# Position bias: for every second group of tiles the first layer is a sum of two small tables, made on GpSimd

## The chip, the cores and the metric

The kernel runs on one core of a Trainium2 chip. The metric is the device time of one execution in microseconds (us). The engines are called PE (TensorE), DVE (VectorE), ACT (ScalarE), POOL (GpSimd) and SP (SyncE, which issues most DMAs here).

## The reference, cut to what matters

Four network layers are computed one after the other. The change touches only the first, an attention with deformed sampling and a learned position bias. The bias of a query pixel (y, x) towards a key position j goes through a small network of three layers with 128 channels:

```python
pos = grid_q[:, :, None, :] - grid_kv[:, None, :, :]
bias = jnp.sign(pos) * jnp.log1p(jnp.abs(pos))
bias = jax.nn.relu(bias @ cpb_w1 + cpb_b1)      # 2 -> 128
bias = jax.nn.relu(bias @ cpb_w2 + cpb_b2)      # 128 -> 128
bias = (bias @ cpb_w3 + cpb_b3).reshape(b, GROUPS, H * W, Hd * Wd)
```

There are 2 x 8 groups with 64 keys each, so 1024 keys, and 32 x 32 query pixels: about a million positions. Since `pos` has one part that depends on x alone and one that depends on y alone, the first layer before its rectification is the sum of a function of x and a function of y, for each key and channel.

## The kernel before, in words

`layer0_sampling` computes the key positions. DVE builds the differences U (L333), ACT takes their absolute value, logarithm and sign (L234 to L237), and DVE multiplies (L337) and splits the result into three bf16 parts (L342 to L351), which are added up as rows of POS, with POSX for the x axis. At the same time POOL makes products for the sampling (L149).

`layer0_bias` is the stage of the change. A tile is 128 channels x 512 positions: one key and one half of the pixels. Four tiles are a quad (their four keys lie in the four row groups of 32 partitions), and eight quads (32 tiles, 16 keys) are an iteration; there are 64 iterations. In each quad:

- PE makes the first layer for four tiles with four products of 32 rows each, into the four banks of z1 (L479). They read EXP, which POOL fills with one addition for four quads, the "spread" (L430).
- ACT rectifies each z1 tile, rounded, into R1 (L547, `first_part`), and DVE makes the rest, the rectified z1 less R1, into R2 (L572, `second_part`). R1 and R2 are rings of eight tiles.
- PE makes the second layer of a tile with three products (L492, L493, L495) into one of three banks of z2. Before the first it waits until the tile three before it has left its bank.
- z2 is rectified into H2 by ACT (L553) for three tiles of a quad and by DVE (L598) for the third one (t % 4 == 2).
- PE makes the third layer of the quad before (L504, or L513 for the last quad of an iteration), with its results gathered in one bank, zo. Once an iteration DVE reads it out (L578), and SP stores it (L444).

The order of PE in a quad is written out by hand: second layer of the quad's four tiles, third layer of the quad before, then the first layer of the quad two further on, which waits until DVE has made the second parts of the next quad (r2_ready). ACT and DVE work one quad ahead with the first and second parts. On ACT a quad is: first parts of t+4 and t+5, hidden tile t, first parts of t+6 and t+7, hidden tiles t+1 and t+3. On DVE it is: second parts of t+4 to t+7, hidden tile t+2.

Ahead of the loop, POOL makes two spreads and clears W3W (L461) and H2 (L462); DVE then fills W3W's windows (L588); and PE starts the third layer's bank with products of zeros (L522). SP loads the weights of the second layer (L447) and then prefetches 9 MB for later stages.

## Time and profile before

| | us |
|---|---|
| median of 3 runs | 4471.59 |
| lowest and highest of them | 4470.86, 4475.02 |
| the profiled execution, its own time | 4470.45 |
| its span in the profile | 4468.6 |

The page gives the busy time of each engine and its costliest groups; a line number is a line of the kernel. A row of the timeline has the start and the duration in microseconds, the engine, the line, the operation, output<-inputs, the shapes and how many instructions are merged in it, with the idle time before it in brackets. A row of one line's instructions has its shortest, median and longest duration in nanoseconds. The position bias takes the span from about 175 to 2380 us, nearly half of it.

### The profile page before, as it was taken

The numbers are of one execution on the slowest core, as the hardware profiler recorded it, in microseconds if no ns is written. First come the engines' busy times: TensorE is split into PE (matmuls) and PEld (weight loads), VectorE is DVE, ScalarE is ACT, GpSimd is POOL, SyncE is SP. The second block draws the span as 40 slices with busy tenths as digits, with TensorE's granted clock in tenths as the row PEclk, the third lists the DMA queues.
The fourth block names the chain that finished last, engine by engine and source line by source line (L and its number), as shares of the span: only waits on it lengthen the run. The fifth ranks groups of instructions, "written<-read, shape, count | busy, mean of one in ns | idle before, by whom it ended". The sixth has DMA issues, their size and how long they took to land. (4 is left out here: it accounts for less than half of the span.)

```text
span 4468.6 us, 65255 instructions
## 1 busy us (share of the span) xinstructions
PE 3954.4 (88%) x19432; PEld 2398.8 (54%) x19432; DVE 2971.8 (67%) x4247; ACT 2532.4 (57%) x4506; POOL 1223.0 (27%) x848
## 2 busy tenths in 40 slices
PE   2599999999999999999998999669878356969999
PEld 1355555555555555555555777537666232435553
DVE  7777777777777777777776333366888944235552
ACT  3488888888888888888885333222211220113331
POOL 1411111111111111111111445405667610016663
PEclk7799999999999999999999999889889666989999
DMA  1200000000000000000002000118999821363311
GB/s 44 86 2 2 2 2 2 2 2 2 2 2 2 2 2 2 2 2 2 2 2 77 1 0 0 65 41 320 377 376 374 309 82 49 125 155 67 67 39 76
DMA packets 136115, 309.13 MB, mean 69 GB/s; under 512 B 43400, under 2 KB 44424, under 8 KB 135004
## 3 DMA queue, kind: packets, MB, share of 16 engines
q1 hardware_dynamic: 94556, 157.02, 11.3%
q0 software_dynamic: 41472, 151.01, 8.7%
q8 instruction: 47, 0.77, 0.1%
q14 instruction: 40, 0.33, 0.0%
HBM read 228.83 MB, written 78.91 MB: 69 GB/s over the span
## 5 line engine op out<-in xcount | busy, mean ns | idle before, releaser
L572 DVE SCALAR_TENSOR_TENSOR cpb_r<-cpb_z,cpb_r 128x512 fp32r<-128x512 f32 x2052 | 1321.8, 686 | 491.8 <-ACT cpb_r L547 486.0
L547 ACT ACTIVATE cpb_r<-cpb_z 128x512 fp32r<-128x512 f32 x2052 | 1121.1, 604 | 278.0 <-PE cpb_z L479 278.0
L553 ACT ACTIVATE cpb_h<-cpb_z,net_vec 128x512 f32<-128x512 f32 x1536 | 1020.5, 714 | 2.0 <-PE cpb_z L495 2.0
L492 PE MATMUL cpb_z<-cpb_r,cpb_w2a 128*128 128x512 f32 x2048 | 856.7, 418 | 3.0
L493 PE MATMUL cpb_z<-cpb_r,cpb_w2b 128*128 128x512 f32 x2048 | 803.6, 392 | 0.0
L495 PE MATMUL cpb_z<-cpb_r,cpb_w2a 128*128 128x512 f32 x2048 | 797.4, 389 | 0.0
L430 POOL TENSOR_TENSOR cpb_exp<-l0k_posx,l0k_pos 128x1024 bf16 (+1 forms) x130 | 247.6, 1905 | 1966.3 <-PE cpb_z L479 1947.0
L1365 DVE SCALAR_TENSOR_TENSOR dc_acc<-dc_g,dc_wt,dc_acc 128x512 f32<-128x512 f32 x560 | 459.2, 826 | 52.4 <-DMA dc_g<-conv_out,dc_idx 36.9
L492 PEld LDWEIGHTS cpb_z<-cpb_r,cpb_w2a 128*128 128x128 f32 x2048 | 384.1, 188 | 189.8 <-issue 123.3
L504 PE MATMUL cpb_zo<-cpb_h,cpb_w3w 128*32 128x512 f32 x3584 | 477.3, 605 | 0.0
L495 PEld LDWEIGHTS cpb_z<-cpb_r,cpb_w2a 128*128 128x128 f32 x2048 | 385.3, 188 | 85.3
L493 PEld LDWEIGHTS cpb_z<-cpb_r,cpb_w2b 128*128 128x128 f32 x2048 | 385.6, 188 | 61.1
L1099 POOL DMA_INDIRECT dc_g<-conv_out,dc_idx x288 | 326.4, 1133 | 203.1 <-DVE dc_acc L1365 121.0
L598 DVE TENSOR_SCALAR cpb_h<-cpb_z,net_vec 128x512 f32<-128x512 f32 x512 | 379.4, 741 | 0.1
L1245 ACT COPY dc_ys<-dc_py 128x512 f32<-128x512 f32 x144 | 84.6, 588 | 384.6 <-DMA conv_out<-dc_ys 228.0
L1155 PE MATMUL dc_py<-net_conv_w,dc_dh 128*128 128x512 f32 x576 | 234.8, 408 | 65.1 <-ACT dc_ys L1245 57.7
L2013 ACT ACTIVATE net_x<-sa_pb 128x512 f32<-128x512 f32 x256 | 139.2, 595 | 267.8 <-PE sa_pb L1939 267.8
L479 PEld LDWEIGHTS cpb_z<-cpb_exp,l0k_w1p 32*128 32x128 bf16 x2056 | 51.9, 91 | 435.9 <-DVE cpb_r L572 430.7
L1909 POOL TENSOR_TENSOR sa_acc<-sa_acc,net_x 128x512 f32<-128x512 f32 x192 | 240.9, 1278 | 70.9 <-ACT net_x L2013 70.1
L885 POOL TENSOR_TENSOR mlp_wb<-l_w,mlp_wa 128x512 fp32r<-128x512 f32 x128 | 194.4, 1539 | 181.8 <-ACT mlp_wa L844 181.8
L2028 DVE TENSOR_REDUCE sa_mxp<-sa_pa 128x1 f32<-128x512 f32 x224 | 144.3, 685 | 147.9 <-PE sa_pa L1923 147.9
L1156 PE MATMUL dc_py<-net_conv_w,dc_dh 128*128 128x512 f32 x576 | 232.8, 404 | 0.0
(320 smaller groups left out, 4884.8 us busy)
## 6 DMA issues: line engine op xcount, KB each, us to landing
conv_out<-dc_ys SPq DMA_DIRECT2D x576, 64.0 KB, 6.2
qk_parts<-gn_r SPq DMA_DIRECT2D x64, 256.0 KB, 2.0
dc_wr<-in_dc_wT SPq DMA_DIRECT2D x9, 1024.0 KB, 5.9
bias_dram<-cpb_bst SPq DMA_DIRECT2D x520, 8.0 KB
net_x<-in_x SPq DMA_DIRECT2D x8, 1024.0 KB, 8.7
sa_qa<-qk_parts SPq DMA_DIRECT2D x16, 512.0 KB
sa_ka<-qk_parts SPq DMA_DIRECT2D x16, 512.0 KB
dc_g<-conv_out,dc_idx POOLq DMA_INDIRECT x288, 7.9
```

Source lines behind the costliest of these rows:

```text
L430: eng.tensor_tensor(EXP[:, slot].rearrange("p (y x) -> p y x", x=W), POSX[:, group, :].broadcast_to([P, H, W]), POS[:, group, :].rearrange ...
L492: pe.matmul(z2[:, bank, :], W2A[:], R1[:, k, :], start=True, stop=False)
L493: pe.matmul(z2[:, bank, :], W2B[:], R1[:, k, :], start=False, stop=False)
L495: pe.matmul(z2[:, bank, :], W2A[:], R2[:, k, :], start=False, stop=True).then_inc(z2_ready, 1)
L504: mm = pe.matmul(zo[32 * r:32 * r + 32, :], W3W[:, half * 4 + c, :], H2[:, (quad * 4 + r) % 8, :], start=(quad == 0), stop=False)
L547: act.activation(R1[:, t % RING, :], z1[:, t % 4, :], ACT.Relu).then_inc(r1_ready, 1)
L553: act.activation(H2[:, t % 8, :], z2[:, t % 3, :], ACT.Relu, bias=V("cpb_b2")).then_inc(h2a, 1)
L572: v.scalar_tensor_tensor(R2[:, t % RING, :], z1[:, t % 4, :], 0.0, R1[:, t % RING, :].bitcast(F32), ALU.max, ALU.subtract).then_inc(r2_rea ...
L598: v.tensor_scalar(H2[:, (t + 2) % 8, :], z2[:, (t + 2) % 3, :], V("cpb_b2"), 0.0, ALU.add, ALU.max).then_inc(h2v, 1)
L1099: pool.indirect_dma_start(out=G[:, u % GR, y, :], out_offset=None, in_=table[tap % SLOTS][b], in_offset=bass.IndirectOffsetOnAxis(ap=IDX[: ...
L1365: v.scalar_tensor_tensor(o, G[:, u % GR, k // 2, (k % 2) * C:(k % 2 + 1) * C], WT[:, k, col:col + 1], DCB[:] if tap == 0 and k == 0 else o ...
L1909: pool.tensor_tensor(acc, ET[:, 0, u, :] if k == 1 else acc, ET[:, k, u, :], ALU.add).then_inc(added, 1)
```

## The change

Quads 0, 2, 4 and 6 of an iteration keep the product on PE. For quads 1, 3, 5 and 7 the tile before the rectification is made on POOL: `SUM[c, y, x] = TAB_x[c, x] + TAB_y[c, y]`, a 128x512 f32 addition with both operands broadcast. The steps:

- In the sampling stage the logarithms stay in U[0] (the split goes on in U[1]), and SP stores their y rows for all keys to DRAM (`log_dram`) with eight DMAs.
- For each iteration SP loads the 16 rows that it needs, broadcast over all 128 partitions, into LOG (256 KB). POOL makes tables from it, by two small operations for each half of an iteration (slot): times the weight of x plus the bias, and times the weight of y.
- Four sums for each odd quad follow on POOL. SUM has the same place in SBUF as R2: a sum's slot may be written once the second layer of the tile that used the slot is complete (z2_ready). Then ACT reads the sum, and DVE reads it and R1, and writes R2 over the sum.
- The order on POOL in an iteration is: sums of quad 3, spread of slot 0, sums of quad 5, table of slot 0, sums of quad 7, spread of slot 1, sums of the next iteration's quad 1, table of slot 1. Ahead of the loop there are two tables and the sums of quad 1, before the two clears.
- PE's first layer is made for even quads only, with no wait for r2_ready. The order of the quads in an iteration (half, slot, j) is changed, so that odd quads are those of the second key half j.

```diff
+            sp.wait_ge(pos_step, 6)
+            for r in range(4):
+                for a in range(2):
+                    row = 32 * r + 16 + 8 * a
+                    sp.dma_start(g["log_dram"].rearrange("n r a x -> r a n x")[r, a].unsqueeze(0), U[0][row:row + 1]
+                                 ).then_inc(log_out, 16)
...
-                    v.tensor_tensor(U[0], U[0], UB[:], ALU.subtract).then_inc(pos_step, 1)
+                    v.tensor_tensor(U[1], rest, UB[:], ALU.subtract).then_inc(pos_step, 1)
...
-        R1, R2 = s.sb("r1", [P, RING, NF], F32R), s.sb("r2", [P, RING, NF], F32R)
+        R1 = s.sb("r1", [P, RING, NF], F32R)
+        with ExitStack() as room:
+
+            SUM = Scope(nc, room, "cpb").sb("sum", [P, RING, NF])
+        R2 = s.sb("r2", [P, RING, NF], F32R)
+        LOG, TAB = s.sb("log", [P, 2, 4, 2, W]), s.sb("tab", [P, 2, 4, 2, W])
...
-            c, half = divmod(quad, 2)
-            return half, c // 2, c % 2, c
+            slot, rest = divmod(quad, 4)
+            half, j = divmod(rest, 2)
+            return half, slot, j, slot * 2 + j
+
+        def on_pe(t):
+
+            return t // 4 % 2 == 0
+
+        def first_layer(t):
+            return z1[:, t % 4, :] if on_pe(t) else SUM[:, t % RING, :]
...
+            def logs(i):
+
+                sp.dma_start(LOG[:], g["log_dram"][i].rearrange("(o s) r a x -> o (s r a x)", s=2).broadcast_to([P, 512])
+                             .rearrange("p (s r a x) -> p s r a x", s=2, r=4, a=2)).then_inc(log_in, 16)
+
             sp.dma_start(W2F[:], d["cpb_w2"]).then_inc(w_in, 16)
+            logs(slice(0, 2))
+            sp.wait_ge(tables, 2)
+            logs(slice(2, 4))
             g["prefetch"](sp)
             with sp.Fori(0, ITERS) as i:
                 sp.wait_ge(staged, i + 1)
                 store(bass.ds(i, 1))
+                sp.wait_ge(tables, i * 2 + 4)
+                logs(bass.ds((i + 2) % ITERS * 2, 2))
...
+            def table(slot):
+
+                pool.nop(nofuse=True)
+                pool.tensor_scalar(TAB[:, slot, :, 0, :], LOG[:, slot, :, 0, :], V("cpb_w1", 0), V("cpb_b1"),
+                                   ALU.mult, ALU.add).then_inc(table_step, 1)
+                pool.tensor_scalar(TAB[:, slot, :, 1, :], LOG[:, slot, :, 1, :], V("cpb_w1", 1), None, ALU.mult
+                                   ).then_inc(tables, 1)
+
+            def sums(i, quad, table_count, consumed):
+
+                half, slot, _, _ = quad_of(quad % QUADS)
+                pool.wait_ge(table_step, table_count)
+                pool.wait_ge(tables, table_count)
+                for r in range(4):
+                    if consumed is not None:
+                        pool.wait_ge(z2_ready, consumed + r)
+                    pool.tensor_tensor(SUM[:, 4 + r, :].rearrange("p (y x) -> p y x", x=W),
+                                       TAB[:, slot, r, 0, :].unsqueeze(1).broadcast_to([P, NF // W, W]),
+                                       TAB[:, slot, r, 1, half * 16:half * 16 + 16].unsqueeze(2).broadcast_to([P, NF // W, W]),
+                                       ALU.add).then_inc(sum_ready, 1)
+
             for slot in range(2):
                 spread(pool, slice(slot, slot + 1), slot)
+            pool.wait_ge(log_in, 16)
+            table(0)
+            table(1)
+            sums(0, 1, 1, None)
             pool.memset(W3W[:], 0.0).then_inc(win_zero, 1)
             pool.memset(H2[:, 4:8, :], 0.0).then_inc(win_zero, 1)
...
-                pool.wait_ge(z1_ready, i * QUADS + QUADS // 2)
+                sums(i, 3, i * 2 + 1, i * TPI + 5)
+                pool.wait_ge(z1_ready, i * 4 + 2)
                 spread(pool, bass.ds(nxt * 2, 1), 0)
-                pool.wait_ge(z1_ready, i * QUADS + QUADS)
+                sums(i, 5, i * 2 + 2, i * TPI + 13)
+                pool.wait_ge(log_in, i * 16 + 32)
+                pool.wait_ge(sum_ready, i * 16 + 8)
+                table(0)
+                sums(i, 7, i * 2 + 2, i * TPI + 21)
+                pool.wait_ge(z1_ready, i * 4 + 4)
                 spread(pool, bass.ds(nxt * 2 + 1, 1), 1)
+                sums(i, 9, i * 2 + 3, i * TPI + 29)
+                pool.wait_ge(sum_ready, i * 16 + 16)
+                table(1)
...
-            pe.wait_ge(r2_ready, 4)
-            layer1(1)
...
-                    if quad + 2 == QUADS // 2:
-                        pe.wait_ge(exp_ready, i * 2 + 2)
-                    if quad + 2 == QUADS:
-                        pe.wait_ge(exp_ready, i * 2 + 3)
-                    pe.wait_ge(r2_ready, i * TPI + quad * 4 + 8)
-                    layer1((quad + 2) % QUADS)
+                    if quad % 2 == 0:
+                        if quad + 2 == QUADS // 2:
+                            pe.wait_ge(exp_ready, i * 2 + 2)
+                        if quad + 2 == QUADS:
+                            pe.wait_ge(exp_ready, i * 2 + 3)
+                        layer1((quad + 2) % QUADS)
...
-                act.activation(R1[:, t % RING, :], z1[:, t % 4, :], ACT.Relu).then_inc(r1_ready, 1)
+                act.activation(R1[:, t % RING, :], first_layer(t), ACT.Relu).then_inc(r1_ready, 1)
...
-                v.scalar_tensor_tensor(R2[:, t % RING, :], z1[:, t % 4, :], 0.0, R1[:, t % RING, :].bitcast(F32),
+                v.scalar_tensor_tensor(R2[:, t % RING, :], first_layer(t), 0.0, R1[:, t % RING, :].bitcast(F32),
                                        ALU.max, ALU.subtract).then_inc(r2_ready, 1)
```

## Rows read from the trace of the kernel before

**Rows 1.** The page's first part: busy time, share of the span, instructions.
```profile
PE 3954.4 (88%) x19432; PEld 2398.8 (54%) x19432; DVE 2971.8 (67%) x4247; ACT 2532.4 (57%) x4506; POOL 1223.0 (27%) x848
```

**Rows 2.** Stretches: length, busy PE, PEld, DVE, ACT, POOL, PE clock, DMA share, GB/s.
```profile
1000.00:2000.00 1000.00, 998.60 (x5612) 569.17 (x5611) 775.71 (x1198) 890.41 (x1637) 112.35 (x59) 1.00 0.01 2
```

**Rows 3.** Timeline of PE in one quad and the start of the next.
```profile
999.98 0.50 PE L492 MATMUL cpb_z<-cpb_r,cpb_w2a 128*128 128x512 f32 x1
...
1000.56 0.39 PE L495 MATMUL cpb_z<-cpb_r,cpb_w2a 128*128 128x512 f32 x1
...
1002.93 1.07 PE L504 MATMUL cpb_zo<-cpb_h,cpb_w3w 128*32 128x512 f32 x8
...
1003.93 0.40 PE L479 MATMUL cpb_z<-cpb_exp,l0k_w1p 32*128 32x512 bf16 x4
...
1004.25 0.50 PE L492 MATMUL cpb_z<-cpb_r,cpb_w2a 128*128 128x512 f32 x1
...
1005.05 0.40 PE L492 MATMUL cpb_z<-cpb_r,cpb_w2a 128*128 128x512 f32 x1
```

**Rows 4.** ACT in the same quad, and the page's group of a copy from SBUF.
```profile
1000.11 1.09 ACT L547 ACTIVATE cpb_r<-cpb_z 128x512 fp32r<-128x512 f32 x2 [0.47 <-PE cpb_z L479]
...
1002.60 1.30 ACT L553 ACTIVATE cpb_h<-cpb_z,net_vec 128x512 f32<-128x512 f32 x2
...
L844 ACT CAST mlp_wa<-l_w 128x512 fp32r<-128x512 f32 x128 | 72.7, 615 | 0.0
```

**Rows 5.** DVE in the same quad, and the durations of all of L572.
```profile
1000.74 1.29 DVE L572 SCALAR_TENSOR_TENSOR cpb_r<-cpb_z,cpb_r 128x512 fp32r<-128x512 f32 x2 [0.76 <-ACT cpb_r L547]
...
1003.50 0.74 DVE L598 TENSOR_SCALAR cpb_h<-cpb_z,net_vec 128x512 f32<-128x512 f32 x1
...
L572 DVE SCALAR_TENSOR_TENSOR cpb_r<-cpb_z,cpb_r x2052: 678/683/692, 181.4 to 2376.5; 128x512 fp32r<-128x512 f32 x187
```

**Rows 6.** POOL's spreads: two on the timeline, and all of the line.
```profile
195.96 1.90 POOL L430 TENSOR_TENSOR cpb_exp<-l0k_posx,l0k_pos 128x1024 bf16 x1 [15.19 <-PE cpb_z L479]
...
1000.27 1.91 POOL L430 TENSOR_TENSOR cpb_exp<-l0k_posx,l0k_pos 128x1024 bf16 x1 [15.06 <-PE cpb_z L479]
...
L430 POOL TENSOR_TENSOR cpb_exp<-l0k_posx,l0k_pos x130: 1901/1904/1979, 174.9 to 2369.6; 128x1024 bf16 x128, 128x1024 bf16<-128x1024 bf16 x2
```

**Rows 7.** POOL's additions of 512 f32: one line's durations, two in a row.
```profile
L1909 POOL TENSOR_TENSOR sa_acc<-sa_acc,net_x x192: 1256/1278/1298, 4012.6 to 4401.6; 128x512 f32<-128x512 f32 x192
...
2454.91 2.52 POOL L885 TENSOR_TENSOR mlp_wb<-l_w,mlp_wa 128x512 fp32r<-128x512 f32 x2
```

**Rows 8.** Timeline of DVE and POOL where both read two SBUF inputs; L902's durations.
```profile
140.50 6.44 DVE L348 SCALAR_TENSOR_TENSOR l0k_pos<-smp_ub,net_vec,l0k_pos 128x4096 bf16<-128x4096 bf16 x1
142.62 6.56 POOL L149 TENSOR_TENSOR net_x<-smp_hx,smp_hya 128x1024 f32<-128x1024 f32 x1
...
157.85 4.49 DVE L348 SCALAR_TENSOR_TENSOR l0k_pos<-smp_ub,net_vec,l0k_pos 128x4096 bf16<-128x4096 bf16 x1
...
2449.85 1.73 POOL L885 TENSOR_TENSOR mlp_wb<-l_wo,mlp_wa 128x512 fp32r<-128x512 f32 x1
...
2450.36 1.77 DVE L902 TENSOR_TENSOR mlp_ab<-l_q,mlp_aa 128x512 fp32r<-128x512 f32 x1
2451.54 1.72 POOL L885 TENSOR_TENSOR mlp_wb<-l_wo,mlp_wa 128x512 fp32r<-128x512 f32 x1
...
L902 DVE TENSOR_TENSOR mlp_ab<-l_q,mlp_aa x16: 679/1546/1772, 2448.1 to 2771.4; 128x512 fp32r<-128x512 f32 x16
```

**Rows 9.** Timeline ahead of the loop: POOL, DVE and PE.
```profile
176.80 0.23 DVE L581 CAST cpb_w2a<-cpb_w2f 128x128 fp32r<-128x128 f32 x1 [2.16 <-DMA cpb_w2f<-in_cpb_w]
...
178.72 0.31 POOL L461 MEMSET cpb_w3w<- 128x256 f32 x1
...
178.97 1.80 POOL L462 MEMSET cpb_h<- 128x2048 f32 x1
...
184.50 0.80 PE L492 MATMUL cpb_z<-cpb_r,cpb_w2a 128*128 128x512 f32 x1
```

More of the change, by code:

```diff
@@ L113, in layer0_sampling @@
         W1B = s.sb("w1b", [P, 3, P], BF16)
+        log_out = s.sem("log_out")
         pos_step, pos_abs, pos_ln, pos_sgn, w1_step = (s.sem("pos_step"), s.sem("pos_abs"), s.sem("pos_ln"),
@@ L135, in _ @@
             sp.dma_start(W1F[:], d["w1rows"]).then_inc(w_in, 16)
+            sp.wait_ge(pos_step, 6)
[4 more added lines that the diff above has]
+                                 ).then_inc(log_out, 16)
+            sp.wait_ge(log_out, 16 * 8)
         @block.gpsimd
@@ L340, in _ @@
             for part in range(3):
+                rest = U[min(part, 1)]
                 v.wait_ge(pos_step, n)
-                v.tensor_copy(UB[:], U[0]).then_inc(pos_step, 1)
+                v.tensor_copy(UB[:], rest).then_inc(pos_step, 1)
                 n += 1
@@ L403, in layer0_bias @@
         h2_free = s.sem("h2_free")
+        log_in, table_step, tables, sum_ready = s.sem("log_in"), s.sem("table_step"), s.sem("tables"), s.sem("sum_ready")
         staged = s.sem("bias_staged")
@@ L454, in _ @@
             sp.wait_ge(stored, 16 + 128 * (ITERS + 1))
+            sp.wait_ge(log_in, 16 * (ITERS + 2))
             g["prefetch_done"](sp)
@@ L544, in first_part @@
             def first_part(i, t):
-                if t % 4 == 0:
-                    act.wait_ge(z1_ready, i * QUADS + t // 4 + 1)
-                act.activation(R1[:, t % RING, :], z1[:, t % 4, :], ACT.Relu).then_inc(r1_ready, 1)
+                if not on_pe(t):
+                    act.wait_ge(sum_ready, i * (TPI // 2) + t // 8 * 4 + t % 4 + 1)
+                elif t % 4 == 0:
+                    act.wait_ge(z1_ready, i * (QUADS // 2) + t // 8 + 1)
+                act.activation(R1[:, t % RING, :], first_layer(t), ACT.Relu).then_inc(r1_ready, 1)
             def hidden(i, t):
@@ L2143 @@
 WEIGHT_COLUMNS = [("bn1_g", 4), ("bn1_b", 4), ("bn2_g", 4), ("bn2_b", 4), ("out_b", 4), ("mlp_b1", 16), ("mlp_b2", 4),
-                  ("off_dw_b", 1), ("off_dw_w", 36), ("off_pw_w", 2), ("cpb_b2", 1), ("cpb_w3", 1), ("cpb_b3", 1),
+                  ("off_dw_b", 1), ("off_dw_w", 36), ("off_pw_w", 2), ("cpb_b2", 1), ("cpb_w3", 1), ("cpb_b3", 1), ("cpb_w1", 2), ("cpb_b1", 1),
                   ("pw_b", 4), ("off_b", 1), ("dw_w", 18), ("dw_b", 2), ("a_dw_w", 18), ("a_dw_b", 2), ("a_pw_b", 4),
@@ L2206, in lay_out @@
          "off_pw_w": both(i["L0_off_pw_w"].T), "cpb_b2": i["L0_cpb_b2"].reshape(P, 1), "cpb_w3": i["L0_cpb_w3"].reshape(P, 1),
-         "cpb_b3": every(i["L0_cpb_b3"]),
+         "cpb_b3": every(i["L0_cpb_b3"]), "cpb_w1": i["L0_cpb_w1"].T, "cpb_b1": i["L0_cpb_b1"].reshape(P, 1),
          "off_b": np.concatenate([np.pad(i["L1_off_b"], (0, 14)).reshape(32, 1)] * 4),
@@ L2254, in build @@
             g["W1P"] = k.sb("w1p", [P, 2, P], BF16, side="right")
+            g["log_dram"] = nc.dram_tensor("log_dram", (P, 4, 2, W), F32).ap()
             layer0_sampling(nc, d, g)
```

## The prediction

> **What bounds the kernel now.** I read the page's busy shares first, then the stretches of time, then the costliest groups of instructions, and last the timeline of two quads, engine by engine. PE is busy for 88% of the span [rows 1]. Inside the position bias it is busy for 998.60 of 1000 us, at the full clock (PEclk 1.00), while DVE has 776, ACT 890 and GpSimd (POOL) 112 [rows 2]. A busy PE need not be a late PE, so the timeline must confirm it. A quad (4 tiles) begins with the first second-layer product (L492) at 999.98 and the next at 1004.25, 4.27 us later; in it PE runs 12 second-layer products, then the third layer (L504) from 1002.93, then the first layer (L479) of a later quad from 1003.93 to 1004.25 [rows 3]. There is no hole between these. So here a microsecond taken off PE is a microsecond gained, as long as no other engine is late.
>
> How late may they be? ACT works through 4 rectifications (L547) and 3 hidden activations (L553), is done at 1003.90, and has waited 0.47 us for the first layer before it began [rows 4]. DVE makes 4 second parts (L572, about 0.60 us apart) and one hidden tile (L598), done at 1004.24 [rows 5]. That last one matters: z2 has 3 banks, so PE's second tile of the next quad (L492 at 1005.05 [rows 3]) waits for it. It comes 0.81 us ahead of its use. POOL only makes one spread in two quads of four (L430), 1.90 us each, and waits 15 us between them [rows 6].
>
> The spreads begin at 195.96 and 2369.6, with 127 distances of four quads between [rows 6]: 2173.6 / 127 = 17.115 us, or 34.23 us for an iteration of 8 quads; there are 64 iterations.
>
> **What PE loses.** In each of the 4 odd quads of an iteration the group L479 goes. From its start to the next L492 is 0.32 us (1003.93 to 1004.25 [rows 3]); I use 0.33 for the small changes at the edge of the loop. 4 x 0.33 = 1.32 us, so PE alone would take 32.91 us for an iteration. This is 64 x 1.32 = 84 us for the kernel. The first L492 behind the group lasts 0.50 where the next lasts 0.40 [rows 3]; whether this 0.10 stays I can't see. So the bounds for a group are 0.22 and 0.42 us: 56 and 108 us in all.
>
> The Trainium skill (TensorE: Matmul & The Clock Gate, Part 3, "Measured speedup vs the span model") gives four row tiles one product's duration plus 4 ns a tile; with the 216 ns that the page gives for the gap of 512 columns that would be an estimate of 0.23 us a group and 59 us in all. The trace has 0.32, so 84 stands.
>
> A second thing gets looser: the first layer no longer waits for DVE, since only even quads use z1, and ACT need not wait its 0.47 us for it. ACT may start a quad's rectifications about 0.4 us earlier. DVE's last result of a quad would then, undisturbed, come some 0.25 us earlier: about 1.05 us ahead of its use.
>
> **What POOL gets.** Sixteen sums of 128x512 f32 for an iteration. The nearest rows are POOL's additions of that size: 1.278 us alone (L1909) and two in 2.52, so one every 1.25 [rows 7]. The spread is an addition with the same kind of broadcast operands; its 1024 bf16 elements take 1.904 [rows 6]. Half of that is 0.95, and a shorter one pays its start in full, so I set the low bound at 1.02; 1.28 is the high one. I take 1.2, between them and nearer to the row of the same size and type. A group of four then takes 5 us of the 8.2 us of two quads. With two spreads (3.8) and two tables (two operations on 128 elements each, of which the trace has none; between 0.1 and 0.3 us each by the small memset of 0.31 us, [rows 9]) POOL needs 16 x 1.2 + 3.8 + 0.8 = 24 us of 33. By its own work it isn't the bound. ACT now reads the sum from SBUF: L844 does such a rounding copy in 615 ns against about 600 of L547 (two in 1.09, the second begun 0.49 after the first) [rows 4], nothing to speak of.
>
> **The cost that isn't in the diff.** For odd quads L572 reads both inputs, the sum and R1, from SBUF; before, one was in PSUM. What the trace shows of such operations beside POOL: in the sampling stage L348, with two SBUF inputs, takes 4.49 us when POOL is idle and 6.44 beside L149, and L149 itself then lasts 6.56 [rows 8]; that is one whole operation waiting for the other, in turns. In the MLP the same is seen at 512 columns: POOL's L885 begins at 2449.85 and 2451.54, and the L902 of DVE between them takes 1.77 us where the shortest L902 takes 0.679 [rows 8]. So while both have work they alternate, a pair takes 1.69 us, of which POOL's part is 1.13 and DVE's 0.56. With one input in PSUM there is no such wait: L572 lasts 692 ns at most in the whole stage, though 128 spreads run in it [rows 5, 6].
>
> This is what the Trainium skill (SBUF — State Buffer, "Who interferes with whom") states: a DVE instruction with two SBUF inputs contends with a GpSimd one that reads SBUF, and who comes second is blocked entirely. It speaks against this change, and the trace agrees with it.
>
> **Does it fall together?** I follow two quads. Zero is PE's start of an even quad (L492); the odd quad before started at -3.94, and the next starts at +4.27. SUM lies in R2's place, so a sum may be written only after z2 of the same slot is complete. The first z2 of a quad is complete 0.97 us after its start (1000.56 + 0.39 [rows 3]), thus at -2.97; POOL wakes some 0.2 us later: of the same product ACT makes use at 1000.11 [rows 4] and the spread at 1000.27 [rows 6]. With 1.2 us each the sums end at -1.56, -0.36, +0.84, and the fourth is still to come. ACT's last hidden tile of the odd quad can begin when that quad's last z2 is complete, at -0.9; the first rectification follows it 0.58 later and lasts 0.6, so R1 of the first odd tile is there at +0.27, and DVE wants its second part then: it waits for the third sum, ends at 1.40. The fourth sum ends at 2.5, the second of DVE at 3.05. In two of four such cases (quads 2 and 6) the program order of POOL has a spread right behind the fourth sum: it ends at 4.8 (1.90 less 0.12, by which a sum that had to wait is shorter too, 1.13 against 1.25). DVE's third ends at 5.35, its fourth at 5.95, the hidden tile at 6.6. PE wants that tile at 4.27 + 0.80 = 5.07. PE stands for 1.5 us.
>
> Where a table stands in the spread's place (quads 4 and 0) it costs DVE 0.2 to 0.5 us, within the 1.05 of room, all the more since PE's halt just before gave POOL a lead. So: 32.91 + 2 x 1.5 = 35.9 us for an iteration, against 34.23. That is +1.68 x 64 = +107 us.
>
> **Prologue.** POOL now makes the tables and four sums ahead of the two memsets that end at 180.77, and PE's first second-layer product (184.50) hangs on these through the window copies [rows 9]: 1 + 5 us later, less the first layer of quad 1 that PE made there (0.5): +5 us. The DMAs: eight small stores of the logarithms go once DVE has made them, ahead of the L348 at 140.50 [rows 8], and have over 30 us until the sampling stage ends; one broadcast load of 256 KB per iteration is issued half an iteration before its use, behind eight 8 KB stores on SP's queue; for the first load of that queue DVE waits 2.16 us here [rows 9]. Should such a load be late once, behind the prefetch, that is some us, not more. DVE's sampling instructions keep their count and size.
>
> **Sum.** The profiled execution took 4470.45 us, 1.1 below the median. 4470.45 + 107 + 5 = 4583.
>
> **Rivals.**
> 1. PE stays the bound. The blocks don't reach PE: if the sum's broadcast operands left the port free for DVE, or if DVE took its four second parts in one go before POOL got in. Then 4470.45 - 84 + 5 = 4391. It decides where the blocks on DVE in one quad come to less than the 1.05 us of room. Against it: in [rows 8] each waits for the other in turn, and one spread alone holds for 1.8.
> 2. The stall feeds itself. With sums of 1.25 us all times above move: DVE's third part ends at 5.54, and the first sum of the next group, whose z2 is complete at 5.24, asks at 5.45, is first, and DVE's fourth part ends at 7.2, the hidden tile at 7.9. PE stands for 2.8 us twice: 32.91 + 5.6 = 38.5, and 4470.45 + 4.28 x 64 + 5 = 4749. It decides at a sum of about 1.23 us.
> 3. Short stalls. With 1.02 us a sum the spread ends at 4.1 and the hidden tile at 5.9: 0.8 us of stall, 34.5 for an iteration, 4493; with 0.66 us of stall gain and loss cancel, near 4475.
> 4. The waits chain over quads (tables too, or z2 of the hidden tile holds ACT), 1 us in each of four pairs beyond case 2: over 4800.
>
> **Chances.** The forecast, stalls of 0.9 to 1.9 us: 0.44. Rival 2: 0.19. Rival 3's slow part (over 0.2%, 4481): 0.06, and its even part 0.07. Rival 1: 0.19, rival 4: 0.05. A measurement of this kernel can tell some 0.2% from no change (its runs lie within 0.1%). Slower 0.44 + 0.19 + 0.06 + 0.05 = 0.74, the same 0.07, faster 0.19. The range reaches from rival 1 to rival 2, 4385 to 4755, since each has nearly 0.2; rival 4 is outside. The forecast's own range is 4510 to 4640.
>
> **What would show it.** In the profile after: L572 has two durations, 0.69 for even and 1.2 to 2.4 us for odd quads; the spread and the sums lengthen from 1.9 and 1.25 to about 2.4 and 1.7 when they meet it; PE has idle time before L492 with the hidden tile of DVE (L598's successor) as its releaser, once in four quads; the spread's distance grows from 17.1 to 18 us. If L572 stays at 0.69 everywhere, the blocking was wrong and 4391 comes; if it is blocked and PE has no idle time, my room for the hidden tile was too small. If a group of sums is late for ACT itself, ACT would show a wait for POOL, which I don't expect.

## The result and the profile after

| | before | after |
|---|---|---|
| median of 4 runs, us | 4471.23 | 4528.04 |
| lowest and highest | 4469.62, 4475.02 | 4524.75, 4529.16 |
| profiled execution | 4470.45 | 4528.95 |
| span | 4468.6 | 4526.8 |

The ratio is 1.0122, with a 95% interval of 1.0106 to 1.0138: the change costs 57 us. The page's first part and the stretch inside the position bias (length, busy PE, PEld, DVE, ACT, POOL, PE clock, DMA share, GB/s) stand against [rows 1, 2]:

```profile
PE 3905.6 (86%) x18404; PEld 2361.8 (52%) x18404; DVE 3276.8 (72%) x4247; ACT 2586.5 (57%) x4506; POOL 2581.7 (57%) x2136
```

```profile
1000.00:2000.00 1000.00, 954.46 (x5030) 539.10 (x5028) 896.16 (x1172) 893.67 (x1599) 710.62 (x628) 1.00 0.03 10
```

PE has 1028 matmuls less over the span: an iteration needs 176 of them instead of 192. A millisecond of the stage holds 5030 against 5612, and that is fewer iterations too (28.6 against 29.2), because PE stands for 45 us of it. DVE keeps its number of instructions in the span and is busy for 305 us more, all of it in the second parts of the sums. The next rows are groups of the page (busy us, mean ns of one, idle time before and its releaser), then the durations of the spread (shortest, median, longest, in ns), and what PE waited for between 200 and 2400 us:

```profile
L509 POOL TENSOR_TENSOR cpb_sum<-cpb_tab 128x512 f32<-128x512 f32 x1028 | 1051.2, 1049 | 653.7 <-PE cpb_z L563 653.7
L640 DVE SCALAR_TENSOR_TENSOR cpb_r<-cpb_sum,cpb_r 128x512 fp32r<-128x512 f32 x1024 | 992.7, 1017 | 158.6 <-ACT cpb_r L615 158.6
L640 DVE SCALAR_TENSOR_TENSOR cpb_r<-cpb_z,cpb_r 128x512 fp32r<-128x512 f32 x1028 | 648.3, 680 | 75.7 <-ACT cpb_r L615 75.1
```

```profile
L453 POOL TENSOR_TENSOR cpb_exp<-l0k_posx,l0k_pos x130: 1902/2354/2357, 175.0 to 2425.5; 128x1024 bf16 x128, 128x1024 bf16<-128x1024 bf16 x2
```

```profile
PE cpb_z L560 <- DVE cpb_h L666: 100.7, 126, 0.8
```

The second part (L572 before, L640 now) takes 680 ns with z1 from PSUM and 1017 on average with the sum from SBUF. The spread (L430, now L453) went from 1904 to 2354. PE's first second-layer product (L492, now L560) waits for DVE's hidden tile (L598, now L666) 126 times in the 63 iterations of this stretch, twice in each, 0.8 us a time. These are three of the signs that the prediction named. Here is one of the two quads: the row of its four sums, DVE and POOL in order of time (the first POOL row there is the fourth sum), and then PE:

```profile
1002.58 4.07 POOL L509 TENSOR_TENSOR cpb_sum<-cpb_tab 128x512 f32<-128x512 f32 x4 [2.49 <-PE cpb_z L563]
...
1005.60 1.05 POOL L509 TENSOR_TENSOR cpb_sum<-cpb_tab 128x512 f32<-128x512 f32 x1
1006.00 1.20 DVE L640 SCALAR_TENSOR_TENSOR cpb_r<-cpb_sum,cpb_r 128x512 fp32r<-128x512 f32 x1 [0.22 <-ACT cpb_r L615]
1006.61 2.35 POOL L453 TENSOR_TENSOR cpb_exp<-l0k_posx,l0k_pos 128x1024 bf16 x1
1007.12 2.39 DVE L640 SCALAR_TENSOR_TENSOR cpb_r<-cpb_sum,cpb_r 128x512 fp32r<-128x512 f32 x1
1009.43 0.68 DVE L640 SCALAR_TENSOR_TENSOR cpb_r<-cpb_sum,cpb_r 128x512 fp32r<-128x512 f32 x1
1010.04 0.68 DVE L640 SCALAR_TENSOR_TENSOR cpb_r<-cpb_sum,cpb_r 128x512 fp32r<-128x512 f32 x1
1010.64 0.74 DVE L666 TENSOR_SCALAR cpb_h<-cpb_z,net_vec 128x512 f32<-128x512 f32 x1
```

```profile
1009.75 0.50 PE L560 MATMUL cpb_z<-cpb_r,cpb_w2a 128*128 128x512 f32 x1
1010.08 0.40 PE L561 MATMUL cpb_z<-cpb_r,cpb_w2b 128*128 128x512 f32 x1
1010.32 0.39 PE L563 MATMUL cpb_z<-cpb_r,cpb_w2a 128*128 128x512 f32 x1
1011.51 0.49 PE L560 MATMUL cpb_z<-cpb_r,cpb_w2a 128*128 128x512 f32 x1 [0.80 <-DVE cpb_h L666]
```

Read the DVE row at 1007.12: an instruction of 0.68 us lasts 2.39, because the spread began 0.5 us ahead of it. The fourth sum had held the second part before it (1.20) in the same way. The two add 0.52 + 1.71 = 2.23 us to DVE's instructions. Not all of it delays the hidden tile, since DVE would have waited for ACT ahead of its third second part anyway. With the late spread of the first experiment the same quad's hidden tile ends 4.27 us behind the quad's start, here 5.91 (1005.47 to 1011.38), 1.64 later. PE wants it 5.08 behind the start, so it is 0.83 late. PE goes on at 1011.51; unhindered it would have gone on at 1010.55 ([rows 3]: the second tile's product starts 0.80 behind the first). The halt costs 0.96, and the next product starts 0.33 later instead of 0.23: 1.07 in all.

The halts account for the time. On PE the quads start at 1001.53, 1005.47, 1009.75, 1014.76 and 1019.04, so four quads take 17.51 us and an iteration 35.02. That is 34.23 - 4 x 0.34 + 2 x 1.07. 64 x (35.02 - 34.23) = 51; the first second-layer product starts at 189.80 instead of 184.50 [rows 9], 5.3 more: 56, of 57 measured between the medians and 58 between the profiled executions.

### The profile page after: what moved, and what is told of

It reads as the page before. It is cut to its first block and busy times, and to the rows that moved or that the text cites. A ratio compares the mean times of both kernels' runs of the same rounds, so it can differ in the third digit from the quotient of the medians.

```text
span 4526.8 us, 66811 instructions
## 1 busy us (share of the span) xinstructions
PE 3905.6 (86%) x18404; PEld 2361.8 (52%) x18404; DVE 3276.8 (72%) x4247; ACT 2586.5 (57%) x4506; POOL 2581.7 (57%) x2136
## 5 line engine op out<-in xcount | busy, mean ns | idle before, releaser
L509 POOL TENSOR_TENSOR cpb_sum<-cpb_tab 128x512 f32<-128x512 f32 x1028 | 1051.2, 1049 | 653.7 <-PE cpb_z L563 653.7
L640 DVE SCALAR_TENSOR_TENSOR cpb_r<-cpb_sum,cpb_r 128x512 fp32r<-128x512 f32 x1024 | 992.7, 1017 | 158.6 <-ACT cpb_r L615 158.6
L560 PE MATMUL cpb_z<-cpb_r,cpb_w2a 128*128 128x512 f32 x2048 | 871.9, 426 | 102.3 <-DVE cpb_h L666 102.3
L563 PE MATMUL cpb_z<-cpb_r,cpb_w2a 128*128 128x512 f32 x2048 | 800.4, 391 | 0.0
L640 DVE SCALAR_TENSOR_TENSOR cpb_r<-cpb_z,cpb_r 128x512 fp32r<-128x512 f32 x1028 | 648.3, 680 | 75.7 <-ACT cpb_r L615 75.1
L615 ACT ACTIVATE cpb_r<-cpb_z 128x512 fp32r<-128x512 f32 x1028 | 561.0, 604 | 144.4 <-PE cpb_z L547 144.4
L560 PEld LDWEIGHTS cpb_z<-cpb_r,cpb_w2a 128*128 128x128 f32 x2048 | 383.7, 187 | 490.9 <-issue 273.5
L615 ACT ACTIVATE cpb_r<-cpb_sum 128x512 fp32r<-128x512 f32 x1024 | 590.2, 633 | 2.9 <-POOL cpb_sum L509 2.9
L572 PE MATMUL cpb_zo<-cpb_h,cpb_w3w 128*32 128x512 f32 x3584 | 477.3, 605 | 0.0
L666 DVE TENSOR_SCALAR cpb_h<-cpb_z,net_vec 128x512 f32<-128x512 f32 x512 | 378.0, 738 | 0.0
L453 POOL TENSOR_TENSOR cpb_exp<-l0k_posx,l0k_pos 128x1024 bf16 (+1 forms) x130 | 305.0, 2347 | 19.3 <-POOLq L65 19.3
L1223 PE MATMUL dc_py<-net_conv_w,dc_dh 128*128 128x512 f32 x576 | 235.2, 408 | 63.0 <-ACT dc_ys L1313 44.0
```

The source lines that it names most:

```text
L453: eng.tensor_tensor(EXP[:, slot].rearrange("p (y x) -> p y x", x=W), POSX[:, group, :].broadcast_to([P, H, W]), POS[:, group, :].rearrange ...
L509: pool.tensor_tensor(SUM[:, 4 + r, :].rearrange("p (y x) -> p y x", x=W), TAB[:, slot, r, 0, :].unsqueeze(1).broadcast_to([P, NF // W, W]) ...
L560: pe.matmul(z2[:, bank, :], W2A[:], R1[:, k, :], start=True, stop=False)
L563: pe.matmul(z2[:, bank, :], W2A[:], R2[:, k, :], start=False, stop=True).then_inc(z2_ready, 1)
L572: mm = pe.matmul(zo[32 * r:32 * r + 32, :], W3W[:, half * 4 + c, :], H2[:, (quad * 4 + r) % 8, :], start=(quad == 0), stop=False)
L615: act.activation(R1[:, t % RING, :], first_layer(t), ACT.Relu).then_inc(r1_ready, 1)
```

## The experiments

The line numbers of a kernel move by two or three with an edit. On the same chips, beside these kernels, the kernel before took 4470.8 to 4474.3 us (medians). The theory: a spread, or a sum, blocks DVE's second part whenever both read SBUF, and two of these in a row, sum and spread, use up the room before PE needs DVE's hidden tile. Rivals: GpSimd's writes are what holds DVE; the sums are too long wherever the spread stands; or the gain of a faster version comes from the edits around the change and not from the product that PE no longer makes.

**The spread, put behind DVE's work**

```diff
                 pool.wait_ge(z1_ready, i * 4 + 2)
+                pool.wait_ge(r2_ready, i * TPI + 16)
                 spread(pool, bass.ds(nxt * 2, 1), 0)
```

and the same with `+ 32` at the other spread. 

> POOL waits with each of the two spreads of an iteration until DVE has made the four second parts of the odd quad (r2_ready); all else is as in the changed kernel. Theory A (the spread holds the SBUF read port while DVE waits with a second part, so that DVE's hidden tile comes late and PE stands, 1.07 us in two quads of an iteration): the halts go, the iteration falls from 35.02 to 32.88 us, 64 x 2.14 = 137 us less than 4528: 4391 us. No second part stays longer than 1.3 us. Theory B (the port's total use, or reading two SBUF inputs as such, makes the loss): as many sums, spreads and second parts share the port as before, so nothing is gained: over 4510 us.

Measured: 4416.56 us (4415.71 to 4418.67), ratio 0.9873 (0.9856 to 0.9889). It is the same work in the same program order on each engine; one wait turned 1.2% slower into 1.3% faster. The longest second part lasts 1.57 us, where the expectation had 1.3 at most. The halts behind the spread are gone, the spread starts right behind DVE's fourth second part and takes its undisturbed time:

```profile
1001.60 1.90 POOL L453 TENSOR_TENSOR cpb_exp<-l0k_posx,l0k_pos 128x1024 bf16 x1 [2.73 <-DVE cpb_r L642]
```

In this run the first of the four second parts still meets the fourth sum, and the quad (it starts at 997.69) shows what room there is without a spread in the way:

```profile
1001.22 0.74 DVE L668 TENSOR_SCALAR cpb_h<-cpb_z,net_vec 128x512 f32<-128x512 f32 x1
...
1002.77 0.40 PE L562 MATMUL cpb_z<-cpb_r,cpb_w2a 128*128 128x512 f32 x1
```

The hidden tile ends at 1001.96, 0.81 us ahead of its use, as before the change.

```profile
1022.78 0.49 PE L562 MATMUL cpb_z<-cpb_r,cpb_w2a 128*128 128x512 f32 x1 [0.38 <-DVE cpb_h L668]
```

```profile
PE cpb_z L562 <- DVE cpb_h L668: 11.3, 30, 0.4
```

The last two fences are PE's one remaining wait, once in an iteration, and its sum over 1000 us. It is why this came to 4417 and not to 4391: z2 has three banks, and 32 tiles aren't a multiple of three, so tile 0 follows tile 30 (DVE's hidden one) in its bank at a distance of two tiles, not three. Before the change the same place cost only about 0.1 us (one quad of 4.39 us, from 1004.25 to 1008.64, among those of 4.27).

**No spread at all** (EXP keeps the first two slots' contents)

```diff
-                spread(pool, bass.ds(nxt * 2, 1), 0)
+                pool.sem_inc(exp_ready, 1)
```

> The two spreads inside the loop are left out (EXP keeps the keys of the first iteration, so the first layer of even quads is computed from the wrong keys). Theory A: the same as with the late spread, 4391 us within 5, since a spread that meets no second part costs nothing. Theory B: the port is relieved of 3.8 us of some 32 in an iteration, so the time falls below that of the late spread: by up to 64 x 3.8 = 240 us if the port were the bound.

Measured: 4415.16 us, 1.4 below the late spread. So a spread that doesn't meet DVE's second parts costs nothing, and neither does the waiting for it. Only its place was wrong.

**Writes alone** (each sum replaced by two clears of 0.53 us)

```diff
-                    pool.tensor_tensor(SUM[...], TAB_x, TAB_y, ALU.add).then_inc(sum_ready, 1)
+                    pool.memset(JUNK[:, r, :], 0.25)
+                    pool.memset(SUM[:, 4 + r, :], 0.5).then_inc(sum_ready, 1)
```

> Each sum is replaced by two clears of 512 columns on POOL, which write SBUF and read nothing and last about 1.04 us together (the values of odd quads are constants, so the bias is wrong). The spreads stay as they are. Theory A with the read side of the port as what is shared: the clears block no second part, so the first one of each group isn't held (it was, by about 0.5 us), the one that meets the spread still is (2.4 us); PE's halt shrinks from 1.07 to about 0.5 us, 4455 us. If writes block too: as the changed kernel, 4528 us.

Measured: 4461.71 us. DVE beside two of the clears, where the sums would have stood:

```profile
1006.94 0.53 POOL L512 MEMSET cpb_sum<- 128x512 f32 x1
1007.13 1.29 DVE L640 SCALAR_TENSOR_TENSOR cpb_r<-cpb_sum,cpb_r 128x512 fp32r<-128x512 f32 x2 [0.61 <-ACT cpb_r L615]
```

Two second parts in 1.29 us: unblocked, with both inputs in SBUF. It isn't the writes, and it isn't the two SBUF inputs by themselves. The spread, which reads, still blocks, and its halts remain, smaller: 0.3 us of waiting each instead of 0.8, since no sum holds the second part ahead of it. The Trainium skill (SBUF — State Buffer, "Who interferes with whom") says that a DVE instruction with two SBUF inputs contends with a GpSimd one that reads SBUF and not with one that only writes; these rows agree.

**The sums without any reader** (the kernel before, with the sums made beside it into a tile that nobody reads)

```diff
+                sums(i, 0, 0, 1, i * TPI + 5)
                 pool.wait_ge(z1_ready, i * QUADS + QUADS // 2)
                 spread(pool, bass.ds(nxt * 2, 1), 0)
```

> The kernel before, to which POOL's sums are added at the same places (gated by the same second-layer products, sixteen an iteration, 1.05 us each), but into a buffer that nobody reads: ACT and DVE take every tile from PSUM. Theory A: a second part with one input in PSUM doesn't share the port, so no second part lasts over 0.70 us and the time is that of the kernel before, 4471 us within 5. Theory C (POOL's work slows its neighbours whatever they read): second parts over 0.7 us and more than 4480 us.

Measured: 4470.34 us, no change. DVE's hidden tile and second parts with z1 in PSUM don't feel 1024 sums, which themselves are never held:

```profile
L591 DVE SCALAR_TENSOR_TENSOR cpb_r<-cpb_z,cpb_r x2052: 678/682/694, 181.4 to 2376.8; 128x512 fp32r<-128x512 f32 x187
```

So POOL's added load costs nothing by itself. What costs is that the sum lies in SBUF and DVE has to read it there.

**Longer sums** (of two plain tiles of constants)

```diff
-                    pool.tensor_tensor(SUM[...], rows of TAB repeated, column of TAB repeated, ALU.add)
+                    pool.tensor_tensor(SUM[:, 4 + r, :], FLAT[:, 0, :], FLAT[:, 1, :], ALU.add)
```

> The changed kernel, but each sum adds two plain f32 tiles of 512 columns that hold constants, in place of the broadcast tables (so the odd quads of the bias are wrong). It asks for the term that was mis-sized: the sum took 1.05 us where the prediction had 1.2. If broadcast operands are what makes it shorter, the plain sum takes 1.25 to 1.28 as the additions of the kernel before do, and the time is that of the long chain: by the prediction's reckoning at 1.25 us a sum, with the halts' 0.27 us that it left out, the halts are 1.9 to 3.0 us in place of 1.07: 4635 to 4775 us. If the duration isn't from the operands (1.05 stays), 4528 us.

Measured: 4992.24 us, above both expectations. The first fence has POOL and DVE in the stalled quad, the second PE:

```profile
1005.57 2.35 POOL L454 TENSOR_TENSOR cpb_exp<-l0k_posx,l0k_pos 128x1024 bf16 x1
1008.31 1.28 POOL L510 TENSOR_TENSOR cpb_sum<-cpb_flat 128x512 f32<-128x512 f32 x1 [0.39 <-PE cpb_z L563]
1008.39 1.75 DVE L640 SCALAR_TENSOR_TENSOR cpb_r<-cpb_sum,cpb_r 128x512 fp32r<-128x512 f32 x1
```

```profile
1010.93 0.49 PE L560 MATMUL cpb_z<-cpb_r,cpb_w2a 128*128 128x512 f32 x1 [2.70 <-DVE cpb_h L666]
```

The chain is that of the prediction's rival 2: the next group's first sum starts 0.08 us ahead of DVE's fourth second part, and the hidden tile ends at 1010.80, 7.8 us behind the start of its quad (1002.99), where 7.9 were worked out for sums of 1.25; PE waits 2.70 us. But rival 2 was given 4749. What it left out is in the stretches (length, busy PE, PEld, DVE, ACT, POOL, PE clock):

```profile
1008.00:1010.90 2.90, 0.23 (x2) 0.00 (x0) 2.90 (x4) 2.02 (x4) 1.28 (x1) 1.00 0.00 0
1012.00:1014.50 2.50, 2.50 (x10) 1.52 (x12) 1.94 (x3) 0.73 (x2) 2.50 (x3) 0.50 0.00 0
```

About a microsecond after PE takes up its work again its granted clock is 0.50, that is 1.2 instead of 2.4 GHz. The stalled quad lasts 8.48 us (1007.27 to 1015.75), where an odd quad without a halt has 3.94: 2.86 until PE goes on (at 1010.93 instead of 1008.07), 0.11 for the product behind, and some 1.6 for the slow clock. An iteration takes 41.88 us (999.05 to 1040.93). In the changed kernel, with halts of 0.80, the clock stays at 1.00.

**Which operand makes a sum cheap** (unused sums again, one form for each of the four)

```diff
+                    if r == 0:    tensor_tensor(out, row repeated, column repeated, ALU.add)
+                    elif r == 1:  tensor_tensor(out, plain, column repeated, ALU.add)
+                    elif r == 2:  tensor_tensor(out, row repeated, plain, ALU.add)
+                    else:         tensor_tensor(out, plain, plain, ALU.add)
```

A repeated row has all 32 values of x again for each y; a repeated column has one value 32 times in a row. 

> The kernel before, plus the sums on GpSimd beside it, into tiles that nobody reads; the four sums of a group take four forms: both operands repeated by their access (as in the change), a plain tile plus a column repeated along the rows, a row repeated plus a plain tile, and two plain tiles. Time 4471 us, within 5: nothing waits for them. By the two kernels seen, the first form takes 1.05 us and the last 1.25 to 1.29. If one repeated operand is what makes the sum cheaper, one of the two mixed forms is at 1.05 and the other at 1.25; if it needs both, the two mixed forms lie between or at 1.25.

```profile
L482 POOL TENSOR_TENSOR cpb_junk<-cpb_tab x256: 1049/1049/1053, 192.2 to 2376.2; 128x512 f32<-128x512 f32 x128
L484 POOL TENSOR_TENSOR cpb_junk<-cpb_flat,cpb_tab x256: 1052/1052/1054, 193.2 to 2377.2; 128x512 f32<-128x512 f32 x128
L486 POOL TENSOR_TENSOR cpb_junk<-cpb_tab,cpb_flat x256: 1272/1278/1290, 194.2 to 2378.2; 128x512 f32<-128x512 f32 x128
L488 POOL TENSOR_TENSOR cpb_junk<-cpb_flat x256: 1272/1307/1315, 195.5 to 2379.5; 128x512 f32<-128x512 f32 x128
```

Measured: 4472.85 us. It is one operand alone: with the column, whose element is repeated, the sum takes 1.05 us, whatever the other operand is; with the repeated row and a plain tile it takes 1.28, as two plain tiles nearly do. The spread has a column operand too, and half of it (0.95) was the right row to go by; the additions of [rows 7] have none.

**Longer sums, with the spread put late** (both edits)

```diff
+                pool.wait_ge(r2_ready, i * TPI + 16)
                 spread(pool, bass.ds(nxt * 2, 1), 0)
...
-                    pool.tensor_tensor(SUM[...], rows of TAB repeated, column of TAB repeated, ALU.add)
+                    pool.tensor_tensor(SUM[:, 4 + r, :], FLAT[:, 0, :], FLAT[:, 1, :], ALU.add)
```

> The changed kernel with sums of two plain tiles (1.28 us each, 4992 us when nothing else is changed), and with the spreads put late, behind the second quad's read-out. Four sums and DVE's four second parts of 0.69 us then alternate: 4 x (1.28 + 0.69) = 7.9 us for a pair of quads that TensorE does in 8.2 us, so without a spread there is just room. If the spread beside the sums starts the halts, most are gone: 4400 to 4500 us, and TensorE's granted clock is 1.00 again. If sums of this size alone are too long for the port, the halts stay: over 4700 us.

Measured: 4512.26 us, 480 less than with the spread in its old place. PE in the stretch, and what it waited for:

```profile
1000.00:2000.00 1000.00, 965.90 (x5072) 544.86 (x5068) 930.50 (x1181) 901.66 (x1614) 882.89 (x634) 1.00 0.03 9
```

```profile
PE cpb_z L562 <- DVE cpb_h L668: 22.2, 86, 0.4
PE cpb_z L562 <- ACT cpb_h L623: 11.9, 29, 0.5
```

So the spread in its old place starts the long halts with sums of 1.28 as well, and the clock is 1.00 again. Small ones remain (0.4 us), some now by ACT, which waits for its sums: POOL is busy for 883 of 1000 us. The time lies 12 us above the bounds expected.

**DVE's hidden tile one place earlier**

```diff
                 for t in range(0, TPI, 4):
-                    for k in range(4):
+                    for k in range(3):
                         second_part(i, t + 4 + k)
                     (hidden tile t + 2)
+                    second_part(i, t + 7)
```

> The changed kernel with one edit on DVE: the hidden tile is made behind the third of the four second parts, not behind the fourth. Theory A (what PE stands for in the spread quads is this hidden tile, and nothing else of that quad): it comes 0.6 us sooner, so each halt falls from 1.07 to about 0.47 us, the iteration from 35.02 to 33.8: 64 x 1.2 = 77 us less, 4451 us. Theory D (PE would stand for the fourth second part, or for ACT, instead): no gain, over 4515 us.

Measured: 4449.81 us. PE's waits for DVE in 1000 us fall to 11.5 us in 59 times, 0.2 each.

**Late spreads, and the hidden tile earlier in the last quad of the iteration alone**

```diff
-                    for k in range(4):
+                    for k in range(3 if t == 28 else 4):
                         second_part(i, t + 4 + k)
                     (hidden tile t + 2)
+                    if t == 28:
+                        second_part(i, t + 7)
```

> The kernel with the late spread (4416.6 us) still has a halt of 0.38 us once an iteration, at the first tile of the next one. My reading: 32 tiles don't fill three banks evenly, so tile 0 takes the bank of tile 30, which is DVE's hidden tile of the last quad, only two tiles before; in an odd quad that is 0.34 us shorter this hidden tile is late. Here the hidden tile stands behind the third second part in the last quad of each iteration only. If the reading is right, the halt goes: 0.4 x 64 = 25 us less, 4391 us. If the halt is from the tables or the store of the bias at the iteration's end, it stays: 4416 us.

Measured: 4388.54 us, PE busy for 1000.00 of 1000 us. The 0.38 us at the turn of the iteration are gone, 28 us for 64 iterations; so that was its cause.

**All of it** (late spreads, hidden tile earlier in each quad, and the two clears ahead of the tables in the prologue)

```diff
+            pool.memset(W3W[:], 0.0).then_inc(win_zero, 1)
+            pool.memset(H2[:, 4:8, :], 0.0).then_inc(win_zero, 1)
             pool.wait_ge(log_in, 16)
...
             sums(0, 1, 1, None)
-            pool.memset(W3W[:], 0.0).then_inc(win_zero, 1)
-            pool.memset(H2[:, 4:8, :], 0.0).then_inc(win_zero, 1)
...
+                pool.wait_ge(r2_ready, i * TPI + 16)
                 spread(pool, bass.ds(nxt * 2, 1), 0)
...
-                    for k in range(4):
+                    for k in range(3):
```

> The changed kernel with three edits: spreads wait for DVE's second parts, the hidden tile stands behind the third second part in every quad, and the two clears of W3W and H2 stand before the tables and sums ahead of the loop. Theory A: PE is never late, 32.9 us for an iteration, and the prologue's 5 us come back: 4471.6 - 84 = 4387 us, within 6. Theory B (the port's total use limits): it can't fall below the late spread's 4416 by more than the prologue's 5 us.

Measured: 4385.68 us (4384.84 to 4386.63), ratio 0.9805 (0.9788 to 0.9821).

```profile
1000.00:2000.00 1000.00, 1000.00 (x5351) 579.59 (x5352) 909.13 (x1247) 938.93 (x1703) 754.49 (x669) 1.00 0.03 10
```

```profile
L642 DVE SCALAR_TENSOR_TENSOR cpb_r<-cpb_sum,cpb_r x1024: 673/682/2871, 185.3 to 2286.5; 128x512 fp32r<-128x512 f32 x171
```

It beats the kernel before by 86 us and the changed one by 142. PE starts its quads at 1008.09 and, eight later, at 1041.00: an iteration takes 32.91 us, the number that the prediction gave for PE alone, and the first second-layer product comes at 184.1 again. DVE is still blocked, now and then for over 2 us; it happens where PE doesn't wait for it.

**PE's work given back** (the fastest version, with each product of the first layer that it has issued twice)

```diff
+                        layer1((quad + 2) % QUADS, False)
                         layer1((quad + 2) % QUADS)
```

> The fastest version so far (4386 us) with each first-layer product that it still has (four a quad, in every second quad: 64 x 16) issued twice, so that TensorE does the work that the change took from it, 32 iterations of 8... that is 16 more products an iteration. If TensorE is what bounds this version everywhere, each product costs what one took in the stream, 0.33 us for a row-group set: four sets an iteration, 1.3 us x 64 = +84, 4470 us, the time of the kernel before; at 0.22 us each it would be +56, 4442. If the gain comes from the placed waits alone, the time stays within 10 us of 4386.

Measured: 4446.23 us, 61 above the fastest version, of which its loop has 56.

```profile
1007.42 0.61 PE L549 MATMUL cpb_z<-cpb_exp,l0k_w1p 32*128 32x512 bf16 x8
1007.96 0.50 PE L563 MATMUL cpb_z<-cpb_r,cpb_w2a 128*128 128x512 f32 x1
```

From the first of them to the next layer are 0.54 us, where one group takes 0.33: the second costs 0.21, the iteration 33.79 (1007.96 to 1041.75), 0.88 = 4 x 0.22 more. The gain does come from PE's work. The kernel before has the same number of such products and takes 34.23; 0.44 us remain. In the fastest version a quad with a group lasts 4.27 us (1008.09 to 1012.36) and one without 3.94 (1004.15 to 1008.09). So a group that is left out is worth 0.33, of which 0.22 is its columns by the doubled products. The other 0.11 I put down to going over to the first layer's matmuls and back; 4 x 0.11 is the 0.44, though about 0.1 of it can as well be the kernel before's wait at the turn of the iteration. No run separates these two.

**The same edit on the kernel before** (hidden tile one place earlier)

```diff
-                    for k in range(4):
+                    for k in range(3):
                         second_part(i, t + 4 + k)
                     (hidden tile t + 2)
+                    second_part(i, t + 7)
```

> The kernel before with one of the edits of the fastest version alone: DVE's hidden tile behind its third second part instead of behind its fourth. If TensorE alone bounds the kernel before but for the one wait of about 0.1 us an iteration at the turn of the iteration, at most 64 x 0.1 = 7 us are saved: 4464 to 4471 us. If the edit is worth what it was worth in the changed kernel (several tenths of a per cent or more, over 30 us), the gain of the fastest version is not the change's but this edit's: under 4440 us.

Measured: 4664.26 us, ratio 1.0433 (1.0415 to 1.0450). Neither expectation: the edit that saves 78 us in the changed kernel costs 193 in the one before.

```profile
1003.94 0.68 DVE L572 SCALAR_TENSOR_TENSOR cpb_r<-cpb_z,cpb_r 128x512 fp32r<-128x512 f32 x1
```

```profile
1004.68 0.40 PE L479 MATMUL cpb_z<-cpb_exp,l0k_w1p 32*128 32x512 bf16 x4 [0.30 <-DVE cpb_r L572]
```

The fourth second part ends at 1004.62, and PE's first layer, which fills the banks of z1 that it empties, starts at 1004.68, 0.30 us late, in nearly every quad. An iteration takes 37.28 us (1005.24 to 1042.52), 3.05 more: 64 x 3.05 = 195. In the changed kernel z1 belongs to even quads alone, so its banks are empty a whole quad before PE fills them, and DVE may do the hidden tile first. The fastest version's gain therefore isn't that of this edit, which makes the kernel before slower. Its other two edits were not tried there; they put POOL's spread and clears in other places, and in that kernel no second part is held by a spread ([rows 5]).

## Why the prediction was right or wrong

The direction and the mechanism held and the range held the time, but the forecast failed on the size: +112 us forecast, +57 measured. The step that failed is the length of a sum, and with it the order in which POOL and DVE get in.

- **PE saves 1.32 us an iteration.** Right: with the halts gone, an iteration takes 32.91 us, as worked out. The 0.33 for a group splits into 0.22 and 0.11 by the run with the products doubled. It was right to let the trace's 0.32 stand. The estimate of 0.23 from the Trainium skill (TensorE: Matmul & The Clock Gate, Part 3, "Measured speedup vs the span model") is close to the 0.22 that a second group right behind the first costs here.
- **DVE and POOL take turns.** Right, and shown with the clears, which don't block, and with the unused sums, which don't either. A spread held a second part for 2.39 us and was itself stretched to 2.35; 1.2 to 2.4 and 2.4 were named. The sums did not lengthen to 1.7, as the prediction wanted as a sign: all 1028 last 1.04 to 1.05 us, because POOL runs ahead of DVE and none of them is held. In the fastest version, where some are, the longest has 1.51. Nor are all odd quads' second parts held: their median is 0.68, their mean 1.02.
- **The room for the hidden tile.** 1.05 us were given, the trace's 0.81 and some 0.25 for ACT's earlier start. With the late spread the room is 0.81: ACT begins earlier, but DVE's third second part starts 2.3 us behind the start of the quad as before, since ACT's second pair of rectifications still stands behind its hidden tile, which waits for the quad's first z2. The 0.25 weren't there. The forecast's own sum doesn't use them; they went into what was said of the tables and of rival 1.
- **The size of the sum: this is the step that failed.** The sum was taken as 1.2 us, "nearer to the row of the same size and type"; it takes 1.05. The text had the right row beside it, the spread "with the same kind of broadcast operands", and set 1.02 from it as the low bound. The runs of four forms showed that the form of an operand decides and not size and type. In a row the sums follow each other every 1.01 us (four in 4.07). POOL also woke 0.08 us behind the product that it waited for, not 0.2.
- **What followed from it: the order.** The prediction had DVE's first second part wait for the third sum, get in ahead of the fourth, and be held three times in all. In the trace the third sum is over before DVE asks. The fourth starts 0.13 us behind the quad's start, DVE asks at 0.53 (0.27 was worked out), and there are two blocks: the fourth sum and the spread. So the spread ends 3.5 us behind the start of the quad, not 4.8; but three second parts are left behind it, not two. The hidden tile ends at 5.91 where 6.6 was worked out, and the halt is 0.96 and not 1.5. With sums of 1.28 the chain came as the prediction had it.
- **Rival 3, and its luck.** By the prediction's working a sum of 1.02 gives a hidden tile at 5.9, halts of 0.8 us and 4493. The 5.9 is what was measured, in part by luck: that working still has DVE get in ahead of the fourth sum, by 0.02 us (it asks at 0.27, the third sum ends at 0.29). And it would have missed the time by 35 us on the other side. A halt worked out as 0.8 costs PE 1.07: 0.13 us until it sees DVE's signal, and 0.11 because the product behind the halt takes 0.33 until the next instead of 0.23; the rest is that the tile comes 0.83 us late. Two halts, 64 iterations: 2 x 0.27 x 64 = 35.
- **Rival 2** was a real case, but for other operands: with sums of 1.28 it came as described, and its price was too low by 243 us. It had no term for PE's clock behind a long halt, which is about 1.6 x 2 x 64 = 200 of them; the halts of 2.97 us for 2.8 are 22 more, and the rest is open.
- **Rival 1** names what the late spread gives once the halt at the turn of the iteration is gone too: 4391 against 4388.54. The 4385.68 of the fastest version is without the 5 us of the prologue that rival 1 still has. It decides where the blocks don't reach PE, which they don't if the spread begins behind DVE's fourth second part.
- **Tables** cost nothing that reaches PE, as said. But their small operations were taken as 0.1 to 0.3 us each, by a clear; they last 0.44 at the shortest (L496) and 0.59 (L498). In their place DVE gets in two second parts during one small operation (L496 lasts 1.41 us in such a place), so the fourth sum behind it is not followed by a long block.
- **Prologue.** +5 forecast, +5.3 measured. With the two clears first it starts at 184.1 again.

Left open: why an element repeated in a row makes a sum cheaper, whether it would in the first operand too, and the last 2 to 4 us of a kernel's difference, by which the stages behind the position bias differ from one kernel's profile to another's.

## What to carry to other kernels

In these runs work moved to GpSimd cost nothing while DVE kept one of its inputs in PSUM, and whole instructions of waiting once DVE read two from SBUF. In such a case place GpSimd's longest instructions behind DVE's run by a wait, as deliberately as one places the work itself. When a change makes a producer skip every second group, look at which buffers came free earlier, since an order that was harmful before may have become the right one. Size an unknown operation by the row with the same kind of operands, ahead of the row with the same number of elements, and look whether its length decides which engine comes first: here sums of 1.05 and of 1.28 us gave two different orders.

## What the runs showed of the hardware

- A GpSimd addition of 128x512 f32 takes 1.05 us if one operand repeats an element 32 times in a row, 1.28 with a repeated row and a plain tile, 1.25 to 1.3 with two plain tiles; a clear of this size takes 0.53, and an operation on 128 elements per partition 0.44 to 0.60.
- DVE isn't held by a GpSimd instruction that only writes (two second parts in 1.29 us beside clears), and is by one that reads (2.39 us for an instruction of 0.68), when DVE's own two inputs both lie in SBUF. With one of them in PSUM no second part lasts over 0.70 us beside 1024 sums.
- The granted clock of PE fell to 1.2 GHz about a microsecond after the end of a halt of 2.7 us, and stayed at 2.4 with halts of 0.8 us, twice in 35 us.
- A group of four row-tiled products of 32 x 512 costs PE 0.22 us right behind another such group and 0.33 when it stands alone between 128-row products.
